# A graph-network kernel whose message stage is written out group by group, with constant waits in place of engine loops

## What is computed

```
h = concat(x[src], edge_attr)              # 200,000 x 48
h = relu(h @ w1a + b1a) @ w1b + b1b        # summed by dst, divided by the count
f = f * src_norm; agg = segment_sum(f[src], dst); f = 0.9 * agg * dst_norm + 0.1 * feat0   # 10 times
```

## Time and profile before

| | us |
|---|---|
| median of 3 runs without the profiler | 6388.56 (6386.31 to 6389.92) |
| the profiled execution, first to last instruction (span) | 7018.8 |
| of it: before the message stage | 193 |
| message stage | 2598 (193 to 2791) |
| nodes of runs | 212 (2791 to 3003) |
| ten propagation steps | 3984 (3003 to 6987) |

### The profile page before, as it was taken

How to read it: one execution, slowest core, us unless ns; L and a number is a source line. 1 busy time by engine, 2 the same in 40 slices (tenths; PEclk the granted TensorE clock), 3 DMA queues, 4 the chain that set the end, 5 groups by cost and what they waited for, 6 DMA issues and landing times. The chain is left out here.

```text
span 7018.8 us, 211605 instructions
## 1 busy us (share of the span) xinstructions
PE 5576.3 (79%) x85008; PEld 3590.0 (51%) x85008; DVE 4279.1 (61%) x12668; ACT 721.3 (10%) x1695; POOL 1693.3 (24%) x1739
## 2 busy tenths in 40 slices
PE   1455555555555556589999999999999999999998
PEld 1344444444444445446565554656555565656564
DVE  7455555555555557766666666666656666666665
ACT  0122222222222223000000000000000000000000
POOL 5655555555555552500000000000000000000000
PEclk9867676666667767799999999999999999999999
DMA  4322222222222222155545555555555555555554
GB/s 117 77 75 76 76 76 77 75 76 77 79 72 79 72 76 94 27 205 194 200 183 204 192 198 205 189 200 191 201 191 201 191 201 201 189 203 189 197 197 169
DMA packets 442864, 1016.61 MB, mean 145 GB/s; under 512 B 253162, under 2 KB 371914, under 8 KB 387354
## 3 DMA queue, kind: packets, MB, share of 16 engines
q1 hardware_dynamic: 386938, 968.76, 39.0%
q0 software_dynamic: 54944, 33.96, 2.6%
HBM read 838.78 MB, written 176.58 MB: 145 GB/s over the span
## 5 line engine op out<-in xcount | busy, mean ns | idle before, releaser
L1864 PE MATMUL banks_fast<-count_units_fast,feature_parts_fast 128*32 128x512 fp8e3 x70608 | 3826.3, 379 | 31.6 <-DVE count_units_fast L1759 26.9
L1864 PEld LDWEIGHTS banks_fast<-count_units_fast,feature_parts_fast 128*32 128x32 bf16 x70608 | 2146.2, 97 | 1688.5 <-issue 37.5
L1758 DVE TENSOR_SCALAR count_units_fast<-packed_ring_fast 128x512 int32<-128x512 int32 x2949 | 1255.8, 426 | 1429.1 <-PE banks_fast L1864 1398.2
L144 POOL DMA_INDIRECT rows_fast<-row_table,idx_fast x1456 | 1408.5, 967 | 996.9 <-ACT count_stage_fast L1257 563.4
L1759 DVE TENSOR_SCALAR count_units_fast<-packed_ring_fast 128x512 int32<-128x512 int32 x2949 | 1237.2, 420 | 0.0
L1351 PE MATMUL banks_fast<-w1a_b1a_fast,turn_fast 49*128 49x96 f32 x3136 | 374.6, 375 | 810.6 <-ACT turn_fast L1262 589.6
L1223 DVE TENSOR_SCALAR window_place_hot_fast<-iota_wide_fast,local_keys_fast,target_weight_fast 128x196 bf16<-128x196 f16 x3136 | 933.9, 343 | 0.0
L1316 PE MATMUL banks_fast<-window_place_hot_fast,window_src_hot_fast 128*128 128x196 bf16 x3136 | 697.4, 312 | 115.4 <-issue 71.0
L1322 PE MATMUL banks_fast<-window_place_hot_fast,window_src_hot_fast 128*128 128x196 bf16 x3136 | 680.2, 305 | 106.1 <-issue 105.4
L1351 PEld LDWEIGHTS banks_fast<-w1a_b1a_fast,turn_fast 49*128 49x128 f32 x3136 | 294.9, 260 | 917.4 <-issue 497.4
L1316 PEld LDWEIGHTS banks_fast<-window_place_hot_fast,window_src_hot_fast 128*128 128x128 bf16 x3136 | 410.1, 155 | 224.2 <-issue 148.3
(11 more groups left out here) (282 smaller groups left out, 1551.5 us busy)
## 6 DMA issues: line engine op xcount, KB each, us to landing
packed_ring_fast<-edge_counts SPq DMA_DIRECT2D x422, 1792.0 KB, 7.0
edge_counts<-count_stage_fast SPq DMA_DIRECT2D x100, 784.0 KB
running_sums<-run_sums_fast SPq DMA_DIRECT2D x100, 768.0 KB
rows_fast<-row_table,idx_fast POOLq DMA_INDIRECT x1456
rows_fast<-attrs_padded SPq DMA_DIRECT2D x98, 128.0 KB
attrs_padded<-in_edge_attr SPq DMA_DIRECT2D x1, 12500.0 KB
rows_fast<-row_table,src_ends_fast POOLq DMA_INDIRECT x112
row_table<-h_nodes_fast SPq DMA_DIRECT2D x1, 1568.0 KB, 5.2
```

What stands on the lines that cost most here:

```text
L144: pool.indirect_dma_start(out=self.rows[:, r, c, 0:DN], out_offset=None, in_=b.dram.table, in_offset=bass.IndirectOffsetOnAxis(ap=idx[:, c ...
L1758: nc.vector.tensor_scalar(to[..., 0:P // 8], of, NIBBLES, None, ALU.bitwise_and)
L1864: last = nc.tensor.matmul(b.banks[at:at + DN, SWEEP[m % 2], 0:COLS], parts[:, side, j, k * DN:(k + 1) * DN], of_strip.bitcast(FP8), start= ...
```

## The change

All five engine loops of the message stage become Python loops over the 98 groups, so group number, addresses and wait values are plain numbers everywhere. The counting increments `sem_inc(taken)` and `sem_inc(passed)` go, and with them these semaphores, `first_done` and the one-element activation at the head of ACT's loop. The loads, stores, gathers, matmuls and vector instructions, their order on each engine and the semaphores that they raise stay as they are.

```diff
             def step(i, t):
-                g, k, r = i * BATCH + t, i * PAIRS_A_LOOP + t // SLOTS, t % AHEAD_GROUPS
+            def step(g):
+                k, r = g // SLOTS, g % AHEAD_GROUPS
                 pool.wait_ge(turned, (SLOTS + g + 1) * Q)
-                pool.sem_inc(taken, 1)
...
                 pool.wait_ge(indexed, g + 1)
-                pool.sem_inc(taken, 1)
                 for u in range(READS):
                     if u:
                         pool.wait_ge(count_read, (SLOTS + g + 1) * READS - READS // Q + u)
-                        pool.sem_inc(taken, 1)
                     ahead.gather(pool, b, r, idx[:, r, :], range(u * G // READS, (u + 1) * G // READS))
...
-            with pool.Fori(0, n_loops - 1) as i:
-                for t in range(BATCH):
-                    step(i, t)
-            for t in range(BATCH - AHEAD_GROUPS):
-                step(n_loops - 1, t)
+            for g in range(J - AHEAD_GROUPS):
+                step(g)
...
-                at = bass.ds(g * G + c, 1) if not isinstance(g, int) else slice(g * G + c, g * G + c + 1)
+                at = slice(g * G + c, g * G + c + 1)
                 dve.wait_ge(summed, g * RUN_STEPS + (c + 1))
...
-            with act.Fori(0, n_loops) as i:
-                nc.scalar.activation(first_act[:, :], b.zeros[:, 0:1], ACT.Relu).then_inc(first_done, 1)
-                act.wait_ge(first_done, i + 1)
-                act.sem_inc(passed, 1)
+            for g in range(J):
...
                         act.wait_ge(counted, g * READS + (u + 1))
-                        act.sem_inc(passed, 1)
...
-            with pe.Fori(0, n_loops) as i:
+            for g in range(J):
```

More of the change, by code:

```diff
@@ new lines, in _, with read_counts, keep_turned, relu_messages @@
+            for g in range(J):
+                k, s = g // SLOTS, g % SLOTS
+                def read_counts(u):
+                    act.wait_ge(counted, g * READS + (u + 1))
+                    to = stage[:, s, :, 2 * u * WD:(2 * u + 2) * WD].bitcast(U16).rearrange("p j (w a) -> p w j a", a=PAIRS)
+                    of = b.banks[:, C_BANK[u % 4], 0:2 * WC].rearrange("p (w j a) -> p w j a", w=2, a=PAIRS)
+                    nc.scalar.copy(to, of).then_inc(count_read, 1)
+                def keep_turned(q):
+                    act.wait_ge(turned, SLOTS * Q + g * Q + (q + 1))
+                    nc.scalar.copy(turn[:, q % 2, :], b.banks[:, T_BANK, 0:2 * P]).then_inc(turn_read, 1)
+                def relu_messages(q):
+                    act.wait_ge(mixed, 2 * g * Q + 2 * (q + 1))
+                    nc.scalar.activation(sums[:, s, q * QC:(q + 1) * QC, :].rearrange("p (k o) d -> p o k d", o=2),
+                                         b.banks[:, M_BANK:M_BANK + 2, 0:QC // 2 * DH].rearrange("p o (k d) -> p o k d", d=DH),
+                                         ACT.Relu).then_inc(mix_read, 1)
+                keep_turned(0)
+                act.wait_ge(sums_out[s], (k + 1) * 16)
+                for u in range(READS):
+                    q, at = divmod(u, QW // 4)
+                    if at == 0:
+                        relu_messages(q)
+                    if at == 0 and q < Q - 1:
+                        keep_turned(q + 1)
+                    if u == 0:
+                        act.wait_ge(counts_out[s], (k + 1) * 16)
+                    read_counts(u)
@@ new lines, in _, with count, turn_rows, mix @@
+            for g in range(J):
+                pair, s, r_rows, turns = g // SLOTS, g % SLOTS, g % AHEAD_GROUPS, g // AHEAD_GROUPS
+                def count(r):
+                    m = (r // (QW // 2)) % 2
+                    pe.wait_ge(hot, SLOTS * WG + g * WG + 2 * (r + 1))
+                    u, side = divmod(r, 2)
+                    if side == 0:
+                        pe.wait_ge(count_read, g * READS + (u + SLOTS * READS - 3))
+                    for half in range(2):
+                        w = (2 * r + half) % QW
+                        last = nc.tensor.matmul(b.banks[:, C_BANK[u % 4], side * WC:(side + 1) * WC], part_hot[:, m, :, w],
+                                                place_hot[:, m, w, :], start=(half == 0), stop=(half == 1))
+                    if side:
+                        last.then_inc(counted, 1)
+                    for half in range(2):
+                        w = (2 * r + half) % QW
+                        last = nc.tensor.matmul(b.banks[:, S_BANK, half * WC:(half + 1) * WC], part_hot[:, m, :, w],
+                                                place_hot[:, m, w, :], start=False, stop=False, skip_group_check=True)
+                    last.then_inc(hot_used, 1)
+                pe.wait_ge(gathered[r_rows], (turns + 1) * (G * 16))
+                pe.wait_ge(attrs_in[r_rows], (turns + 1) * 16)
+                def turn_rows(q):
+                    for k in range(QC // 2):
+                        c = q * QC + 2 * k
+                        last = nc.tensor.transpose(b.banks[:, T_BANK, k * P:(k + 1) * P],
+                                                   rows[:, r_rows, c:c + 2, :].rearrange("p c d -> p (c d)"), b.ident[:, :])
+                    last.then_inc(turned, 1)
+                def mix(q):
+                    pe.wait_ge(turn_read, g * Q + (q + 2))
+                    pe.wait_ge(mix_read, g * Q + (q + 1))
+                    if q == 0 and s == 0:
+                        pe.wait_ge(local_made, pair * KEY_STEPS + 4)
+                    if q == Q - 1 and s == SLOTS - 1:
+                        next_keys = pair + 1
+                        pe.wait_ge(keys_in[next_keys % AHEAD_GROUPS], (next_keys // AHEAD_GROUPS + 1) * 16)
+                        turn_keys(next_keys % AHEAD_GROUPS)
+                    for k in range(QC):
+                        at = 64 * (k % 2)
+                        last = nc.tensor.matmul(b.banks[:, M_BANK + k % 2, k // 2 * DH:(k // 2 + 1) * DH],
+                                                turn[at:at + DI + 1, q % 2, (k // 2) * P:(k // 2 + 1) * P],
+                                                b.w1a[at:at + DI + 1, :], start=True, stop=True)
+                        if k >= QC - 2:
+                            last.then_inc(mixed, 1)
+                turn_rows(0)
+                for r in range(WG // 2):
+                    q, at = divmod(r, QW // 2)
+                    if at == 0:
+                        mix(q)
+                    if at == 0 and q < Q - 1:
+                        turn_rows(q + 1)
+                    count(r)
```

182 lines of the change are left out of this document (45 added, 137 removed).

## The result

The changed kernel takes 6412.11 us (median of 5 runs, 6409.94 to 6413.75) against 6389.92 us before in the same comparison (6386.31 to 6390.71): 1.0036 times as long, interval [1.0025, 1.0047]. The prediction said 6387.5 us, with a range of 6345 to 6404, and gave a slower kernel 9%.

A forecast was written before the change was run, and what follows sets the result against it. POOL's gathers were taken to bound the message stage in the runs. Terms 0 + 0 + 0 - 0.5, less perhaps another half for DVE's last additions, gave -1 us: 6387.5 us, range 6345 to 6404.

The forecast's parts named there:

- The floor: Message stage: without pauses POOL's gathers and key fetches alone set its length, 20.9 us a group, POOL ending at 2137.1 us.
- the 630 us of pauses: Profiled span 7018.8 us against median 6388.56, 630.2 us less: placed in message-stage pauses that the unprofiled runs lack.
- hand-offs bound the runs: Rival, message stage: the ring PE, ACT, PE sets the pace, so waits and branches count in full; 6325 us, chance 0.18.
- POOL's waits and branches, 0: Message stage, POOL: dropped waits, register computations and five loop branches lie hidden beside gathers already issued; 0 us.
- The -10 us of its branches: Bound for POOL's five loop branches in the message stage, 2.0 us each, if no gathers already issued cover them.
- PE's branches, 0: Message stage, PE: loop branches of 3325 ns and late transposes are made up while POOL gathers; 0 us, bound -17.7 us.
- Longer straight code costs nothing that I can find: Whole kernel: unrolled code adds no cost, since the ten steps already execute their many matmuls in 3984 us.
- Register waits, -0.5: Message stage, PE, ACT, DVE, SP: dropped waits and computations hidden under POOL except in the last group; -0.5 us, bound -46.
- gathers stretched: Rival, message stage: DVE without register computations meets POOL's gathers in denser bursts, 15 ns more each; 6410 us, chance 0.09.
- Branches on the path: Rival, message stage: PE's loop ends are exposed though POOL bounds the rest, -17.7 us; 6371 us, chance 0.09.

## Why the prediction was wrong

**The floor: right, 19 us too low.** It read past the 630 us of pauses, said that POOL's gathers bound the runs, and put POOL's end at 2137.1 us and the stage's between 2150 and 2164. The unchanged kernel profiled again has POOL without a pause, and its last gather ends at 2156; the stage ends at 2170. The gap is mainly the mean of a gather, 982 ns instead of the 967 of the earlier trace rows (1456 x 15 = 22 us); 7 us more of idle time and a start 8 us earlier nearly cancel. The rival "hand-offs bound the runs" (6325 us) is out: POOL idles 443.8 us before and after, and that is the 0.30 us between gathers of the earlier trace rows.

**POOL's waits and branches, 0: right.** With POOL's block put back the time moves by 1.2 us. The -10 us of its branches didn't come.

**PE's branches, 0: right in the message stage, wrong for the kernel.** The slow branch of the earlier trace rows and the late transposes of the earlier trace rows are hidden: with PE's loop back the stage ends no later. "Longer straight code costs nothing that I can find" looked at the number of the steps' matmuls only. The steps got 15.5 us shorter because their code moved. No row of before showed what a move would do, but the idle times with "issue" in the steps would have shown that something was there to gain or lose.

**Register waits, -0.5: the step that failed.** The text put "DVE's address computations" under POOL's cover with all the rest and looked only at what they cost. They also held the wait between two additions on VectorE's sequencer, and this kept gathers short. With them gone a gather costs 26 ns more, +38 us in the stage that POOL bounds; VectorE's block alone makes 38.9. An engine off the critical path set the pace of the one that is on it.

**The rival "gathers stretched": the right mechanism, with 9% and the wrong picture.** It named the place (VectorE beside POOL's gathers), the point from which it decides (9 ns) and the sign to look for (the mean of a gather), and gave 6410 us for 15 ns. Measured were 26 ns and 6412 us, the nearness being luck, since 15 us came back in the steps. It expected denser bursts. VectorE is hardly denser: the additions keep their 0.47 us, and what changed is how often a comparison and a gather stretch each other, 275 times instead of 52. The page of the Trainium skill that it cited, "SBUF — State Buffer", SBUF: two separate sides, says that when a GpSimd operation meets a VectorE operation that needs the shared port pair, the first to start holds the pair for its whole instruction and the other is blocked. The paired rows agree in that both sides get longer at once, 0.94 to 1.10 us and 0.32 to 0.46. The rows don't show which of the two holds what, nor whether the comparison is of the kind that needs the pair, and 0.15 us is less than a whole instruction of either side (0.32 and 0.94).

**Branches on the path (6371 us): out.** Putting PE's block back made the kernel slower, but not by a late message stage.

**What stays open.** Why an addition that carries its own wait sets the comparisons some ns earlier against the gathers, and why so few ns decide, isn't shown: no record in the trace says which engine holds a port. Why the unchanged kernel's gathers (982 ns) are 8 ns longer than those of the changed kernel with VectorE's block put back (974) was not followed up. SP's block was not tried alone; VectorE's alone already makes 38.9 of the 40.5 us.

## What to carry to other kernels

Where POOL's indirect DMAs bound a stage, read the mean of a gather with and without VectorE's dependent chains beside it, and try both places for their waits: on the instruction, and on the sequencer by an increment behind the wait. Removing idle-looking sequencer work from an engine with slack can cost the engine that has none. And when a long stage is unrolled, compare the time of the stages behind it as well: the 0.36% here are the sum of +40 and -15 us in two places.

## What the runs showed of the hardware

**The place of a wait.** Two exchanged lines, with as many instructions, change the mean gather from 1006 to 969 ns and the kernel from 6414.1 to 6359.4 us. The Trainium skill, "Perfetto Trace Analysis", DVE / Act Engine Instruction, describes that a VectorE instruction is pushed with its wait into a queue behind the sequencer, which then goes on; the records agree in so far as an addition's own record carries its wait, while the bare increment ahead of it on the sequencer carries none. That a gather on another engine feels it is this case's finding.

**The place of a loop.** The same ten steps took 3964.9, 3974.8 and 4010.8 us between counter and last branch with 0, 64 and 128 more increments in PE's code far ahead of them. The Trainium skill, "Runtime: NRT & Kernel Launch", Instruction fetch mechanics, says that code is fetched in blocks, that crossing a block is mostly hidden, and that a branch to a block that isn't held stops execution. The 6.9 us branch agrees with the last; the idle times of 1 to 5 us in the steps are a cost that wasn't hidden. The DMA records tie them to code loads: the profile has a queue q8 of the kind "instruction", whose 16 KB packets come every 6.6 us or so in the steps, and each idle time over 0.9 us (8 of them before, 12 with 128 increments) ends 1.2 to 1.9 us after such a packet has landed. Which instructions a packet brought is not shown.
